# x of a chunk loaded in four groups of images, apart from one another, in place of two halves

## The chip, the cores and the metric

The kernel runs on one core of a Trainium2 chip. The metric is the device time of one execution in microseconds. SP is the engine that issues most transfers and computes nothing.

## The reference

```python
def reference(x, ...):                       # x: 32 images, 64 channels, 56 x 56, float32
    x = x + conv_ref(_ln_c(x), ...)          # layer norm over channels, sign, 3x3 conv with sign weights,
                                             # batch norm over images and places, clip to -1..1
    t = tokens of x                          # (32 images, 3136 places, 64 channels)
    t = t + ffn_ref(_ln_t(t), ...)           # 8 experts of three 64x64 layers, ReLU after the first two
    return t as x

def ffn_ref(x, ...):
    feat = jnp.mean(x, axis=0)               # mean over the 32 images, at each place
    w = softmax(feat @ Wr + br)              # one gate for each place and expert
    h = relu(bn(x @ W1[e] + b1[e])); h = relu(bn(h @ W2[e] + b2[e])); y = h @ Wo[e] + bo[e]
    return sum over e of y * w[e]
```

The gate of a place needs the mean over all images, so a chunk of places is worked on with all 32 images at once.

## The kernel before, in words

**First stage.** All images go through the first layer norm, the sign, the convolution and the statistics of its batch norm. The conv's result stays on the chip as `y`.

**Second stage.** 28 chunks (`chunk(k, s, first, left)` on each engine, from `body_of_chunks`). Chunk k holds rows k and 28 + k of all 32 images; the upper half of the rows is on partitions 0 to 63, the lower on 64 to 127, channels along the partitions. `s` is k % 2 and picks one of two buffers; `left` is the number of chunks that follow, 2 at most; `first` is true for k = 0. The images of a chunk are four groups (`g`) of 8. A chunk is 8 units (u), a unit is one half of the experts for one group, and a unit has six points, so a chunk has 48 positions. At fixed positions, given by the table `STEADY`, engines do steps for coming chunks: positions under 48 for chunk k + 2, from 48 on for chunk k + 1.

**The life of x.** SP loads x of chunk k + 2 into `xin[:, s]` while chunk k runs (`load_half`, L280; a half is two groups, and one call issues two transfers, one for each half of the partitions). The buffer holds chunk k's own values until GpSimd has used them, so each load waits for `x1g_done`, which `add_const` (L468: `o` = `xin` + the gates' constant) raises by one for each group. VectorE adds the conv's part into `xin` (`prep`, L1010) at positions 16, 21, 36 and 39 for groups 0 to 3; it waits for `x_loaded` at groups 0 and 2. TensorE centres x over channels (L634), ScalarE squares it into `spread`, TensorE sums (L642), ScalarE and VectorE make the inverse root `rs` (done at position 60, which is 12 of the next chunk).

**The other things that SP carries**, each with its wait: `spread_rs`, the row `rs` to memory (L293, two transfers) and back to all partitions (L297, four); `store(k, g)`, a group of the output (L314, two); `spread_gates`, the gates to memory and back (L304, L307). SP does them strictly in the order in which they are written.

**GpSimd** does `add_const` of groups 0 to 2, `add_upper(k - 1, 3)` (L474, L478: the sums into `o`), `add_const` of group 3 (which waits until `store(k - 1, 3)` has landed), `add_upper(k, 0)`, the two norm multiplications `xc` x `spread` (L446, which raise `u_done[0]` and `u_done[1]`), the feature (L455 to L460, the mean over images that the logits need), `add_upper(k, 1)` and `add_upper(k, 2)`.

**TensorE** runs, a unit, six steps of four concurrent 64x64 matmuls: layer 1 (L575), 2 (L599) and 3 (L614), each twice; at position 37 of a chunk the logits of the next one (L654), later its gates (L661, L675). **ScalarE** takes layer 1 out of PSUM (L801), **VectorE** layer 2 (L993). Once a chunk, near its start, ScalarE writes `gconst` (L846); its starts mark the chunks in the trace.

SP's order before:

```python
def chunk(k, s, first, left):
    if left > 1:
        sp.wait_ge(x1g_done, G * k + 2)
        load_half(k + 2, s, 0)
    if not first:
        store(k - 1, G - 1)
    if left:
        spread_rs(k + 1, 1 - s)
    if left > 1:
        sp.wait_ge(x1g_done, G * k + G)
        load_half(k + 2, s, 1)
    for g in range(G - 2):
        store(k, g)
```

Of the kernel before, what the change touches and what calls it, by code (L numbers as in the profile page):

```python
# [18 lines left out]
RP = H // 2  # L19
# [9 lines left out]
STEPS = 2  # L29
G = 4  # L30
BG = B // G
# [18 lines left out]
def metaformer_kernel(nc, x, cw, gamma, beta, Wr, br, W1, b1, g1, be1, m1, v1, W2, b2, g2, be2, m2, v2, Wo, bo, out):  # L50
    with ExitStack() as ctx:
        def sb(name, shape, dt, to=ctx):
            return to.enter_context(nc.sbuf_tensor(name, shape, dt))

        def sem(name):
            return ctx.enter_context(nc.semaphore(name))
# [40 lines left out]
        h = sb("h", [P, 2, 2, 2, NG], F32)  # L97
# [21 lines left out]
        xin = sb("xin", [P, 2, B, W], F32)  # L119
# [36 lines left out]
        d_bn = sem("d_bn")  # L156
        s_bn = sem("s_bn")

        x_loaded = [sem(f"x_loaded{p}") for p in range(STEPS)]
        t_done = sem("t_done")  # L160
        x1_done = sem("x1_done")
        centre_done = sem("centre_done")
# [13 lines left out]
        u_done = [sem(f"u_done{p}") for p in range(STEPS)]  # L176
# [13 lines left out]
        x1g_done = sem("x1g_done")  # L190
# [45 lines left out]
        def places_at(when, h):  # L236
            return [g for g in range(len(when)) if when[g] == h]
# [13 lines left out]
        with nc.Block() as block:  # L251
# [3 lines left out]
            def _(sp):  # L255
# [18 lines left out]
                for m in range(TWOS):  # L274
                    load_images(m)

                def load_half(q, s, p):
                    images = slice(2 * BG * p, 2 * BG * p + 2 * BG)
                    for h in range(2):
                        sp.dma_start(xin[64 * h:64 * h + 64, s, images], x[images, :, RP * h + q, :].rearrange("b c w -> c b w")).then_inc(x_loaded[p], 16)  # L280

                sp.wait_ge(a_stats, 1)
                for q in range(2):
                    for p in range(STEPS):
                        if q:
                            sp.wait_ge(x_loaded[p], 32)
                        load_half(q, q, p)

                def spread_rs(q, s):

                    sp.wait_ge(rs_done, q + 1)
                    for h in range(2):
                        sp.dma_start(rs_rows[s, h].rearrange("p i n -> (p i) n"), rs[h:h + 97:32, :]).then_inc(rs_kept, 16)  # L293
                    sp.wait_ge(rs_kept, 32 * q)
                    for p in range(STEPS):
                        for h in range(2):
                            sp.dma_start(spread[64 * h:64 * h + 64, p],  # L297
                                         rs_rows[s, h, p:p + 1].broadcast_to([C, 2, NG])).then_inc(rb_loaded[p], 16)

                def spread_gates(q, s):  # L300

                    sp.wait_ge(wT_done, q + 1)
                    for a in range(2):
                        sp.dma_start(gate_rows[s, :, a], wT[E * a:E * a + E, :]).then_inc(gates_kept, 16)  # L304
                    sp.wait_ge(gates_kept, 32 * q)
                    for hi in range(2):
                        sp.dma_start(wb[64 * hi:64 * hi + 64, s].rearrange("p n a w -> p (n a w)"),  # L307
                                     gate_rows[s, PAIRS * hi:PAIRS * hi + PAIRS].rearrange("(o n) a w -> o (n a w)", o=1).broadcast_to([C, NG])).then_inc(wb_loaded, 16)

                def store(k, g):  # L310
                    images = slice(BG * g, BG * g + BG)
                    sp.wait_ge(sum_done, G * k + g + 1)
                    for h in range(2):
                        sp.dma_start(out[images, :, RP * h + k, :].rearrange("b c w -> c b w"),  # L314
                                     o[64 * h:64 * h + 64, images]).then_inc(stored[g], 16)

                def chunk(k, s, first, left):
                    if left > 1:
                        sp.wait_ge(x1g_done, G * k + 2)
                        load_half(k + 2, s, 0)  # L320
                    if not first:
                        store(k - 1, G - 1)
                    if left:
                        spread_rs(k + 1, 1 - s)
                    if left > 1:
                        sp.wait_ge(x1g_done, G * k + G)
                        load_half(k + 2, s, 1)
                    for g in range(G - 2):
                        store(k, g)
                    if left:  # L330
                        spread_gates(k + 1, 1 - s)
                    store(k, G - 2)
                    if not left:
                        store(k, G - 1)
# [550 lines left out]
            def _(dve):  # L885
# [117 lines left out]
                def prep(at, q, s, h):  # L1003
                    Y, Z = L2_BANKS
                    for g in places_at(at.x1, h):
                        if g % 2 == 0:
                            dve.wait_ge(x_loaded[g // 2], 32 * q + 32)
                        dve.wait_ge(t_done, G * q + g + 1)
                        xg = xin[:, s, BG * g:BG * g + BG, :]
                        V.scalar_tensor_tensor(out=xg, in0=t[:, g].rearrange("p (b w) -> p b w", w=W), scalar=2.0, in1=xg,  # L1010
                                               op0=ALU.min, op1=ALU.add).then_inc(x1_done, 1)
# [94 lines left out]
```

## Time and profile before

| | us |
|---|---|
| median of 3 runs | 1347.0 (1344.51 to 1348.73) |
| the profiled execution | 1349.55 |
| its span | 1347.8 |
| TensorE matmul busy | 1287.7 (96%) |
| ScalarE busy | 881.1 (65%) |
| VectorE busy | 817.4 (61%) |
| GpSimd busy | 652.3 (48%) |
| mean granted TensorE clock | 0.989 |

The matmuls' ends are modelled and they overlap one another, so a busy TensorE is not one at its peak. The first stage ends, and the chunks begin, near 190 us. "Idle before" in a row is the engine's idle time just before the instructions of that row, and the name behind it is what ended it; "issue" stands where the profile shows nothing that it waited for.

### The profile page before, as it was taken

How to read it: one execution, taken by the hardware profiler on the slowest of the kernel's cores; microseconds unless marked ns; L12 is line 12 of the kernel's file. 1: busy time of each engine (PE TensorE's matmuls, PEld its weight loads, DVE VectorE, ACT ScalarE, POOL GpSimd, SP SyncE). 2: the span in 40 equal slices, each digit the busy share in tenths (PEclk: the TensorE clock that was granted, in tenths of full speed). 3: DMA queues.
4: the chain of work that ended last, by engine and by line, in shares of the span. 5: the costliest groups of instructions: out<-in, count | busy, mean ns of one | idle time of the engine just before them, and what ended most of it. 6: DMA issues, size and time to landing. Idle time of an engine off the chain costs nothing. (4 is left out here: it accounts for less than half of the span.)

```text
span 1347.8 us, 36336 instructions
## 1 busy us (share of the span) xinstructions
PE 1287.7 (96%) x14692; PEld 672.2 (50%) x14692; DVE 817.4 (61%) x1468; ACT 881.1 (65%) x1122; POOL 652.3 (48%) x580
## 2 busy tenths in 40 slices
PE   5999769999999999999999999999999999999997
PEld 3788525544445445444444544544445555534453
DVE  4444646666656566566665566665665656666654
ACT  5677656666666667666766666676666666666653
POOL 0142414554555544555644555445556455555453
PEclk9999979999999999999999999999999999999999
DMA  9897403343334442333442434423333334344221
GB/s 210 192 197 198 80 14 70 77 84 70 64 70 77 83 91 52 75 77 77 84 86 47 83 65 83 91 58 70 76 77 84 74 59 82 72 81 87 45 48 28
DMA packets 260976, 112.50 MB, mean 83 GB/s; under 512 B 241544, under 2 KB 245216, under 8 KB 260832
## 3 DMA queue, kind: packets, MB, share of 16 engines
q1 hardware_dynamic: 259568, 108.86, 39.5%
q0 software_dynamic: 1264, 1.61, 0.6%
q8 instruction: 104, 1.70, 0.6%
q14 instruction: 40, 0.33, 0.1%
HBM read 84.25 MB, written 26.17 MB: 82 GB/s over the span
## 5 line engine op out<-in xcount | busy, mean ns | idle before, releaser
L993 DVE SCALAR_TENSOR_TENSOR v<-ps,negb,wb 128x448 f32<-128x448 f32 x896 | 573.0, 678 | 413.2 <-PE ps L599 405.1
L801 ACT ACTIVATE h<-ps,bias 128x896 f32<-128x896 f32 x448 | 450.3, 1005 | 280.7 <-PE ps L575 278.0
L614 PE MATMUL ps<-v,wo 64*64 64x448 f32 x3584 | 472.7, 540 | 10.4 <-issue 9.7
L599 PE MATMUL ps<-h,w 64*64 64x448 f32 x3584 | 470.2, 540 | 4.2 <-issue 3.5
L575 PE MATMUL ps<-xc,w 64*64 64x448 f32 x3584 | 468.1, 540 | 6.4 <-issue 6.0
L474 POOL TENSOR_TENSOR sums<-sums 128x448 f32<-128x448 f32 x112 | 127.7, 1140 | 339.7 <-ACT sums L807 339.7
L599 PEld LDWEIGHTS ps<-h,w 64*64 64x64 f32 x3584 | 180.7, 133 | 178.9 <-issue 153.7
L614 PEld LDWEIGHTS ps<-v,wo 64*64 64x64 f32 x3584 | 173.7, 133 | 168.8 <-issue 148.1
L575 PEld LDWEIGHTS ps<-xc,w 64*64 64x64 f32 x3584 | 163.0, 132 | 183.9 <-issue 171.4
L468 POOL TENSOR_TENSOR o<-xin,gconst 128x448 f32<-128x448 f32 x112 | 125.1, 1137 | 206.4 <-DMA out<-o 95.0
L478 POOL TENSOR_TENSOR o<-o,sums 128x448 f32<-128x448 f32 x112 | 127.5, 1139 | 8.8
L446 POOL TENSOR_TENSOR xc<-xc,spread 128x896 f32<-128x896 f32 x54 | 113.3, 2112 | 20.0 <-DMA spread<-rs_rows 19.9
L536 PE MATMUL ps<-sgn,convw 64*64 64x392 bf16 x2304 | 116.8, 330 | 3.7 <-issue 3.7
L932 DVE BATCH_NORM_STATS2 stats<-y 128x6 f32<-128x392 f16 x128 | 66.2, 560 | 78.6 <-ACT y L768 78.5
L807 ACT ACTIVATE sums<-ps 128x896 f32<-128x896 f32 x112 | 101.4, 906 | 17.8 <-PE ps L614 17.8
L536 PEld LDWEIGHTS ps<-sgn,convw 64*64 64x64 bf16 x2304 | 91.0, 107 | 29.1 <-issue 8.9
L1010 DVE SCALAR_TENSOR_TENSOR xin<-t,xin 128x448 f32<-128x448 f32 x112 | 92.3, 825 | 1.6 <-ACT t L825 1.5
L825 ACT ACTIVATE t<-y,bn 128x448 f32<-128x448 f16 x112 | 83.5, 751 | 0.0
L768 ACT ACTIVATE y<-ps 128x784 f16<-128x784 f32 x64 | 52.8, 825 | 43.8 <-PE ps L536 43.8
L816 ACT ACTIVATE xc<-ps 128x896 f32<-128x896 f32 x54 | 49.6, 918 | 27.9 <-PE ps L634 27.9
L521 PE MATMUL ps<-xa,centre 64*64 64x392 f32 x512 | 63.2, 511 | 1.4 <-DMA xa<-in_x 1.3
L634 PE MATMUL ps<-xin,centre 64*64 64x448 f32 x432 | 59.0, 550 | 1.9 <-DVE xin L1010 1.1
(163 smaller groups left out, 626.5 us busy)
## 6 DMA issues: line engine op xcount, KB each, us to landing
xa<-in_x SPq DMA_DIRECT2D x128, 196.0 KB, 5.2
xin<-in_x SPq DMA_DIRECT2D x112, 224.0 KB, 5.0
out<-o SPq DMA_DIRECT2D x224, 112.0 KB, 2.5
spread<-rs_rows SPq DMA_DIRECT2D x108, 224.0 KB, 4.2
wb<-gate_rows SPq DMA_DIRECT2D x54, 112.0 KB, 2.8
rs_rows<-rs SPq DMA_DIRECT2D x54, 7.0 KB
gate_rows<-wT SPq DMA_DIRECT2D x54, 1.8 KB
rows<-in_L_ffn_g POOLq DMA_DIRECT2D x2, 256.0 KB, 5.2
```

Source lines behind the costliest of these rows:

```text
L446: nc.gpsimd.tensor_tensor(xc[:, s, p], xc[:, s, p], spread[:, p], ALU.mult).then_inc(u_done[p], 1)
L468: nc.gpsimd.tensor_tensor(o[:, images, :], xin[:, s, images, :], gconst[:, s:s + 1, :].broadcast_to([P, BG, W]), ALU.add).then_inc(x1g_don ...
L474: nc.gpsimd.tensor_tensor(sums[:, 0], sums[:, 0], sums[:, 1], ALU.add).then_inc(p_sum, 1)
L478: nc.gpsimd.tensor_tensor(og, og, sums[:, 0], ALU.add).then_inc(sum_done, 1)
L536: last = mm(ps[64 * high:64 * high + 64, CONV_BANKS[g % 2] + low, 0:NA], convw[rows_, tap, :], sgn[rows_, slot, top:top + KG, kx:kx + W], ...
L575: last = mm(ps[64 * two:64 * two + 64, L1_BANKS + ab, 0:NG], w1[half, P * q + C * two:P * q + C * two + C], xc[half, s, g // 2, ab ^ (g % ...
L599: last = mm(ps[64 * i:64 * i + 64, L2_BANKS[ab] + low, 0:NG], w2[rows_, Q + QUADS * i, :], h[rows_, u % 2, i, ab, :], start=True, stop=True)
L614: last = mm(ps[64 * par:64 * par + 64, ACC_BANKS + low, 0:NG], wo[rows_, 2 * Q + d, :], v[rows_, u % 2, par ^ (g % 2), d, :], start=(Q == ...
L801: A(h[:, u % 2, i], ps[:, L1_BANKS:L1_BANKS + 2, 0:NG], ACT.Relu, bias=bias[:, 0, q:q + 1]).then_inc(h_done[i], 1)
L807: A(sums[:], ps[:, ACC_BANKS:ACC_BANKS + 2, 0:NG], ACT.Copy).then_inc(sums_kept, 1)
L993: last = V.scalar_tensor_tensor(out=v[:, u % 2, ab, d, :].rearrange("p (b w) -> p b w", w=W), in0=ps[:, L2_BANKS[ab] + d, 0:NG].rearrange( ...
L1010: V.scalar_tensor_tensor(out=xg, in0=t[:, g].rearrange("p (b w) -> p b w", w=W), scalar=2.0, in1=xg, op0=ALU.min, op1=ALU.add).then_inc(x1 ...
```

## The change

x of a chunk is loaded by groups of 8 images (`load_group`, two transfers each) in place of halves of 16, each with a semaphore of its own. SP's order in a chunk is new: group 0 of chunk k + 2 as soon as `add_const(k, 0)` is through; the store of the last group of the chunk before; group 1; `spread_rs`; the store of group 0; group 2; group 3, which waits for `add_const(k, 3)` and also for the second norm multiplication of chunk k + 1 (`u_done[1]`, the last user of what `spread_rs` brings); the store of group 1; the rest as it was. VectorE's x1 step waits for each group's own load.

```diff
--- before.py
+++ after.py
@@ -156,7 +156,7 @@
         d_bn = sem("d_bn")
         s_bn = sem("s_bn")
 
-        x_loaded = [sem(f"x_loaded{p}") for p in range(STEPS)]
+        x_loaded = [sem(f"x_loaded{g}") for g in range(G)]
         t_done = sem("t_done")
         x1_done = sem("x1_done")
         centre_done = sem("centre_done")
@@ -274,17 +274,17 @@
                 for m in range(TWOS):
                     load_images(m)
 
-                def load_half(q, s, p):
-                    images = slice(2 * BG * p, 2 * BG * p + 2 * BG)
+                def load_group(q, s, g):
+                    images = slice(BG * g, BG * g + BG)
                     for h in range(2):
-                        sp.dma_start(xin[64 * h:64 * h + 64, s, images], x[images, :, RP * h + q, :].rearrange("b c w -> c b w")).then_inc(x_loaded[p], 16)
+                        sp.dma_start(xin[64 * h:64 * h + 64, s, images], x[images, :, RP * h + q, :].rearrange("b c w -> c b w")).then_inc(x_loaded[g], 16)
 
                 sp.wait_ge(a_stats, 1)
                 for q in range(2):
-                    for p in range(STEPS):
+                    for g in range(G):
                         if q:
-                            sp.wait_ge(x_loaded[p], 32)
-                        load_half(q, q, p)
+                            sp.wait_ge(x_loaded[g], 32)
+                        load_group(q, q, g)
 
                 def spread_rs(q, s):
 
@@ -315,18 +315,25 @@
                                      o[64 * h:64 * h + 64, images]).then_inc(stored[g], 16)
 
                 def chunk(k, s, first, left):
+
+                    if left > 1:
+                        sp.wait_ge(x1g_done, G * k + 1)
+                        load_group(k + 2, s, 0)
+                    if not first:
+                        store(k - 1, G - 1)
                     if left > 1:
                         sp.wait_ge(x1g_done, G * k + 2)
-                        load_half(k + 2, s, 0)
-                    if not first:
-                        store(k - 1, G - 1)
+                        load_group(k + 2, s, 1)
                     if left:
                         spread_rs(k + 1, 1 - s)
+                    store(k, 0)
                     if left > 1:
+                        sp.wait_ge(x1g_done, G * k + 3)
+                        load_group(k + 2, s, 2)
                         sp.wait_ge(x1g_done, G * k + G)
-                        load_half(k + 2, s, 1)
-                    for g in range(G - 2):
-                        store(k, g)
+                        sp.wait_ge(u_done[1], k + 3)
+                        load_group(k + 2, s, 3)
+                    store(k, 1)
                     if left:
                         spread_gates(k + 1, 1 - s)
                     store(k, G - 2)
@@ -1003,8 +1010,7 @@
                 def prep(at, q, s, h):
                     Y, Z = L2_BANKS
                     for g in places_at(at.x1, h):
-                        if g % 2 == 0:
-                            dve.wait_ge(x_loaded[g // 2], 32 * q + 32)
+                        dve.wait_ge(x_loaded[g], 32 * q + 32)
                         dve.wait_ge(t_done, G * q + g + 1)
                         xg = xin[:, s, BG * g:BG * g + BG, :]
                         V.scalar_tensor_tensor(out=xg, in0=t[:, g].rearrange("p (b w) -> p b w", w=W), scalar=2.0, in1=xg,
```

On SP, one chunk with two or more chunks after it stood so before. `xin` is the load of x, `out` a store of one group, `rs_rows` and `spread` the inverse root to memory and back, `gate_rows` and `wb` the gates:

```order
L280 DMA xin<-in_x 64x16x56 x2
L314 DMA out<-o 64x8x56 x2
L293 DMA rs_rows<-rs 4x448 x2
L297 DMA spread<-rs_rows 64x896 x4
L280 DMA xin<-in_x 64x16x56 x2
L314 DMA out<-o 64x8x56 x4
L304 DMA gate_rows<-wT 8x56 x2
L307 DMA wb<-gate_rows 64x448 x2
L314 DMA out<-o 64x8x56 x2
```

The same chunk on SP in the changed kernel:

```order
L280 DMA xin<-in_x 64x8x56 x2
L314 DMA out<-o 64x8x56 x2
L280 DMA xin<-in_x 64x8x56 x2
L293 DMA rs_rows<-rs 4x448 x2
L297 DMA spread<-rs_rows 64x896 x4
L314 DMA out<-o 64x8x56 x2
L280 DMA xin<-in_x 64x8x56 x4
L314 DMA out<-o 64x8x56 x2
L304 DMA gate_rows<-wT 8x56 x2
L307 DMA wb<-gate_rows 64x448 x2
L314 DMA out<-o 64x8x56 x2
```

Group 1 has moved behind the first store, and groups 2 and 3 behind the store that follows the spread; the row of four `xin` is both of them, with a wait between.

## Rows read from the trace of the kernel before

**Rows 1.** The page, busy time of each engine.

```profile
PE 1287.7 (96%) x14692; PEld 672.2 (50%) x14692; DVE 817.4 (61%) x1468; ACT 881.1 (65%) x1122; POOL 652.3 (48%) x580
```

**Rows 2.** The page, a DMA queue: packets, MB, share of 16 engines.

```profile
q8 instruction: 104, 1.70, 0.6%
```

**Rows 3.** Groups by line: busy us, mean ns, idle before and its releasers.

```profile
L614 PE MATMUL ps<-v,wo 64*64 64x448 f32 x3584 | 472.7, 540 | 10.4 <-issue 9.7 <-ACT sums L807 0.5
L599 PE MATMUL ps<-h,w 64*64 64x448 f32 x3584 | 470.2, 540 | 4.2 <-issue 3.5 <-ACT vareps L829 0.4
L575 PE MATMUL ps<-xc,w 64*64 64x448 f32 x3584 | 468.1, 540 | 6.4 <-issue 6.0
```

**Rows 4.** Line L846: duration ns min/median/max, first and last start us.

```profile
L846 ACT ACTIVATE gconst<-ps x28: 206/208/211, 192.3 to 1300.4; 128x56 f32<-128x56 f32 x28
```

**Rows 5.** Timeline of ScalarE, three chunks' starts: start us, us, instruction.

```profile
317.85 0.21 ACT L846 ACTIVATE gconst<-ps 128x56 f32<-128x56 f32 x1
...
357.10 0.21 ACT L846 ACTIVATE gconst<-ps 128x56 f32<-128x56 f32 x1
...
400.43 0.21 ACT L846 ACTIVATE gconst<-ps 128x56 f32<-128x56 f32 x1
```

**Rows 6.** Timeline of TensorE at 382 us, in brackets the idle before.

```profile
381.87 0.98 PE L614 MATMUL ps<-v,wo 64*64 64x448 f32 x8 [1.96 <-issue]
```

**Rows 7.** Windows: us, busy (count) of PE, PEld, DVE, ACT, POOL, clock, DMA share, GB/s.

```profile
322.00:323.00 1.00, 1.00 (x16) 0.36 (x12) 0.89 (x2) 0.49 (x2) 0.00 (x0) 1.00 0.96 200
...
378.00:379.00 1.00, 1.00 (x19) 0.54 (x16) 0.99 (x2) 0.00 (x0) 1.00 (x2) 1.00 1.35 188
...
380.00:381.00 1.00, 0.00 (x0) 0.00 (x0) 1.00 (x2) 0.88 (x2) 0.87 (x2) 1.00 0.10 13
...
383.00:384.00 1.00, 1.00 (x12) 0.60 (x8) 0.00 (x0) 0.83 (x1) 0.92 (x2) 0.50 0.00 0
```

**Rows 8.** Timeline of SP in the chunk that starts at 317.85.

```profile
320.40 1.73 SPq L280 DMA_DIRECT2D xin<-in_x  x2
326.80 1.30 SPq L314 DMA_DIRECT2D out<-o  x2
329.45 1.10 SPq L293 DMA_DIRECT2D rs_rows<-rs  x2
331.71 2.48 SPq L297 DMA_DIRECT2D spread<-rs_rows  x4
334.24 1.34 SPq L280 DMA_DIRECT2D xin<-in_x  x2
335.87 13.16 SPq L314 DMA_DIRECT2D out<-o  x4
```

**Rows 9.** Line L280 (issue ns, first and last, landing); the page's stores, us to landing.

```profile
L280 SPq DMA_DIRECT2D xin<-in_x x112: 595/672/1423, 136.9 to 1238.4; - x112
...
DMA to landing us min/median/max: 3.5/5.0/6.5
...
out<-o SPq DMA_DIRECT2D x224, 112.0 KB, 2.5
```

**Rows 10.** Timeline of VectorE, the same chunk: groups 1, 2 and 3 of x.

```profile
335.14 1.18 DVE L1010 SCALAR_TENSOR_TENSOR xin<-t,xin 128x448 f32<-128x448 f32 x1
...
347.17 1.03 DVE L1010 SCALAR_TENSOR_TENSOR xin<-t,xin 128x448 f32<-128x448 f32 x1
...
350.83 0.61 DVE L1010 SCALAR_TENSOR_TENSOR xin<-t,xin 128x448 f32<-128x448 f32 x1
```

**Rows 11.** Timeline of GpSimd, the same chunk: sum of group 0, norms, end of the feature.

```profile
334.70 1.14 POOL L478 TENSOR_TENSOR o<-o,sums 128x448 f32<-128x448 f32 x1
336.43 4.29 POOL L446 TENSOR_TENSOR xc<-xc,spread 128x896 f32<-128x896 f32 x2 [0.59 <-DMA spread<-rs_rows]
...
344.98 0.42 POOL L460 TENSOR_TENSOR feat<-feat 128x112 f32<-128x112 f32 x1
```

**Rows 12.** Timeline of TensorE, the same chunk: the logits.

```profile
347.98 0.27 PE L654 MATMUL ps<-wr,feat 64*56 64x8 f32 x5
```

More of the change, by code:

```diff
@@ L318, in chunk @@
                     if left > 1:
-                        sp.wait_ge(x1g_done, G * k + 2)
-                        load_half(k + 2, s, 0)
+                        sp.wait_ge(x1g_done, G * k + 1)
+                        load_group(k + 2, s, 0)
                     if not first:
                         store(k - 1, G - 1)
+                    if left > 1:
+                        sp.wait_ge(x1g_done, G * k + 2)
+                        load_group(k + 2, s, 1)
                     if left:
                         spread_rs(k + 1, 1 - s)
+                    store(k, 0)
                     if left > 1:
+                        sp.wait_ge(x1g_done, G * k + 3)
+                        load_group(k + 2, s, 2)
                         sp.wait_ge(x1g_done, G * k + G)
-                        load_half(k + 2, s, 1)
-                    for g in range(G - 2):
-                        store(k, g)
+                        sp.wait_ge(u_done[1], k + 3)
+                        load_group(k + 2, s, 3)
+                    store(k, 1)
                     if left:
```

## The prediction

> **What bounds the kernel now.** I read the page first: the TensorE is busy for 96% of the span [rows 1], so whatever the change does to the transfers counts only if it moves the TensorE. The part on queues comes next: beside SP's queue there is one, q8, that carries 104 packets of instructions, 1.70 MB, some 16 KB each [rows 2]. The TensorE has by far the longest program, 14692 matmuls and as many weight loads [rows 1], and 29384 instructions in at most 104 blocks are over 280 a block, so most of these blocks must be its code (an inference: the profile does not say whose they are). The grouping by line then shows the three layers' matmuls idle 21 times for 19.2 us in all (9.7 + 3.5 + 6.0) behind "issue", which is no wait that the profile knows [rows 3]. Of semaphore waits these groups have next to none.
>
> The chunk's length says how much is lost. The row of gconst (one a chunk) starts at 192.3 the first and at 1300.4 the last time of 28 [rows 4]: 1108.1 / 27 = 41.04 us a chunk. A clean chunk takes 357.10 - 317.85 = 39.25 us, the next one 400.43 - 357.10 = 43.33 [rows 5]. The same work is done in both. So the 27 intervals lose about 27 x (41.04 - 39.25) = 48 us (the first and the last differ a little in what they hold; I take it as a bound).
>
> Where does the long one lose it? Its TensorE stands for 1.96 us before 381.87, released by "issue" [rows 6]. In the slices before, the DMA engines are at 1.35 of their mean share in 378 to 379; while the TensorE stands, in 380 to 381, they are at 0.10. Two microseconds later the granted clock is 0.50, that is 1.2 GHz in place of 2.4, for some 3 us [rows 7]. I read this so: a block of code was queued behind a long burst of transfers, came late, the TensorE ran dry, and once it was followed by a lower clock. The burst is what SP issues in one go. Of the clean chunk: rs_rows at 329.45, four spread transfers from 331.71, the second half of x from 334.24, the store of group 0 from 335.87 [rows 8]. A store transfer is 112 KB [rows 9]; a spread one (64 partitions of 896 floats) and one of a half of x (64 of 16 images of 56 floats) are 224 KB. That is 4 x 224 + 2 x 224 + 2 x 112 = 1568 KB. The first half of x, alone at 320.40, is moved at a share of 0.96 in 322 to 323 [rows 7, 8], and the chunk loses nothing by it.
>
> **The change part by part, all in the clean chunk's times.**
>
> *More issues.* Eight x transfers of 112 KB a chunk for four of 224 KB, same bytes and same 224-byte pieces. One issue takes 672 ns at the median [rows 9]; a store of 112 KB takes the same, 1.30 us for two [rows 8]. So SP spends 4 x 0.67 = 2.7 us a chunk more. It lies in SP's waits: nothing is lost but what is queued behind, below. The x of the first two chunks is loaded from 136.9 on [rows 9], during the first stage, 55 us before the first gconst at 192.3 [rows 4]: nothing.
>
> *Group 1 goes behind the store of group 3 of the chunk before.* The store is issued from 326.80 to 328.10; group 1 then from 328.10 to 329.44, 8 us later than now. VectorE takes it at 335.14 [rows 10]. What a 112 KB load needs from issue to landing is not in the trace: 2.5 us is the store's of that size, 5.0 the load's of twice that [rows 9]. I take 3.5, between, since an HBM read of half the bytes should lie nearer the store; the second transfer, issued at 328.77, lands by 332.3, with 331.3 and 333.8 as ends. Even the late end leaves 1.3 us. Cost nothing, covered by that slack. VectorE's two more waits a chunk (groups 1 and 3) are met before they are reached.
>
> *rs_rows has group 1 ahead of it.* SP is free again at 329.44 and rs is ready at 329.45, so the issue itself is not moved. But rs_rows, and through its landing the four spreads, now have 224 KB in front. In 322 to 323 a load of x moves 200 GB/s [rows 7], at which 224 KB (0.229 MB) are 1.15 us: 0 to 1.2 us, I take 1. The norm multiplications on GpSimd start at 336.43, at the release of the spread [rows 11], and the feature sum ends at 344.98 + 0.42 = 345.40. TensorE's logits, which want it, run at 347.98 [rows 12]. Slack 2.6 us: 1 us is hidden. Against it, the spread no longer shares the engines with the second half of x. Net on the path: nothing.
>
> *Groups 2 and 3.* Store 0 is issued from 335.87 (it can go no earlier: its sum ends at 334.70 + 1.14 [rows 11]), then group 2 from 337.2 to 338.5; the norms end at 336.43 + 4.29 = 340.72 and let out group 3, issued until 342.1. With 5.0 us to landing as the worst, group 2 is there by 343.0 and group 3 by 346.4; they are taken at 347.17 and 350.83 [rows 10]. Slack 4 us each. Behind group 3 SP holds the store of group 1, whose sum GpSimd makes only after the feature, so after 345.40: nothing.
>
> *The burst.* This is the term that counts. After the spread come 224 KB of store and 224 KB of group 2, issued at the rate of 0.67 us per 112 KB, and group 3 only after 340.7. So the 1568 KB become 896 KB, then 448 KB that trickle, then 224 KB apart, and the stretch with the engines over-full ends with the spread, about 2 to 3 us earlier. A block wanted in that tail is no longer late; one wanted during the spread is as late as now. I take half of the visible idle of the matmuls: 0.5 x 19.2 = 9.6 us. The ends: nothing below (all of the lateness could come from the spread), and 48 us of loss above, of which the tail of the burst can hardly hold more than half, 24.
>
> Here two rules of the skill speak against the term. The Trainium skill, Runtime: NRT & Kernel Launch, Instruction fetch mechanics, has the sequencer fetch 16 KiB blocks of 256 instructions through a queue of its own, "mostly hidden". The size agrees with q8's packets [rows 2]; "hidden" does not agree with the 1.96 us gap, if that gap is a fetch. The Trainium skill, DMA: Bandwidth & Descriptors, Queues, rings and completion order, says that each engine takes turns between queue rows packet by packet; by it a backlog in SP's row would hold the code up by a packet or so, and this term would be 0. Rows 6 and 7 speak for more; no row shows the fetch itself.
>
> *Tail.* From chunk 26 on no x is loaded, and the code is the old one in order: nothing.
>
> **Sum.** The profiled execution took 1349.55 us (span 1347.8), 2.55 above the median of the runs, 1347.0. 1349.55 - 9.6 = 1339.95; against the median, 1347.0 - 9.6 = 1337.4. I say 1337. A measurement of this kernel can tell 0.3%, 4 us, from nothing.
>
> **The rivals.**
>
> *The burst is not what makes the code late, or the spread alone is.* For it: the clean chunk has the same burst and no gap, and the skill's rule of turns. Against it: the gap stands right behind the 1.35 slices. Time: 1347, within 4 us. Chance 0.25.
>
> *The tail is worth more than I take.* If every gap goes, the hidden part of each and the lower clock with it: 1347 - 24 = 1323. This is the low part of the forecast's own case, as likely as a fifth of it.
>
> *Group 1 comes too late (slower).* Place: VectorE at L1010, position 21 of 48 in the chunk, between two v products that TensorE's third layer waits for. Behind it VectorE has nothing else to do and the TensorE drains within a step. It decides once group 1 lands after 335.14, that is 6.4 us after its second issue, or when the store of group 3 is itself held up by 3 us. Price: each microsecond beyond, in 26 chunks; at half a microsecond 13 us, 1360. For it: 8 us of lead are given away, and read and store share the engines. Against it: the longest of all 112 landings of the doubled size is 6.5 us [rows 9]. Chance 0.08.
>
> *More and denser issues hold up the code in a new place (slower).* Store 3, group 1 and rs_rows are now issued without a break from 326.8 to 330.6, and a block wanted there may be late where it wasn't. Price: one gap of half a microsecond in every second chunk, 13 x 0.5 = 6.5 us, with the gain of the tail lost: 1353. For it: the total issue time grows by 2.7 us a chunk. Against it: the DMA engines are mostly idle in that stretch. Chance 0.09.
>
> **How the numbers follow.** The forecast's case has 0.58, "no effect" 0.25, the two slower ones 0.17 together. Where the gain happens it is 5 to 25 us, so 1322 to 1342; the range goes on to the whole of "no effect", 1351, and a microsecond into the second slower rival: 1322 to 1352. What lies outside is a gain over 25 us (0.05) and group 1 late (0.08), with part of the other. Faster by over 0.3%: 0.58; within: 0.25; slower: 0.17.
>
> **What would show it.** Right: the period of gconst falls from 41.04 towards 40.7; the idle of the three matmul groups behind "issue" falls from 19.2 to about 10; slices after the spread show a share below 1.1; no idle of VectorE behind the DMA of x; norms start no later than 1 us after now. Wrong: the same 19 us of idle at other places (second or fourth case); a row of VectorE's L1016 (the x1 step's new line) waiting for the DMA of x (third case); GpSimd's norms over 2.6 us later, with the TensorE idle at the logits.

## The result and the profile after

| | before | changed |
|---|---|---|
| median of 6 runs | 1345.76 us | 1333.27 us |
| lowest to highest | 1342.81 to 1348.73 | 1330.46 to 1336.47 |
| profiled execution, its span | 1349.55, 1347.8 | 1334.76, 1332.6 |

The ratio is 0.9906, with a 95% interval of 0.9887 to 0.9924: 12.5 us less, where 9.6 were forecast. The runs of before are measured anew beside the changed kernel, so their median differs a little from the 1347.0 of the table above.

The page of the changed kernel: busy time of each engine, and the queue of instructions.

```profile
PE 1281.6 (96%) x14692; PEld 661.5 (50%) x14692; DVE 819.3 (61%) x1468; ACT 881.1 (66%) x1122; POOL 652.5 (49%) x580
...
q8 instruction: 104, 1.70, 0.5%
```

The count of matmuls is the same. The span fell by 15.2 us, and the TensorE's busy time by 6.1 of them (1287.7 in [rows 1]), so its idle time fell by 9.1, from 60.1 to 51.0. Of these 15.2 us some 2 are scatter: the profiled execution of before was 3.8 us above its median, the changed one 1.5.

The three layers' matmuls, grouped by line (busy us, mean ns of one, idle us before them and its releaser):

```profile
L621 PE MATMUL ps<-v,wo 64*64 64x448 f32 x3584 | 469.7, 540 | 4.7 <-issue 3.9
L606 PE MATMUL ps<-h,w 64*64 64x448 f32 x3584 | 466.5, 539 | 3.1 <-issue 2.4
L582 PE MATMUL ps<-xc,w 64*64 64x448 f32 x3584 | 463.3, 540 | 5.1 <-issue 4.6
```

Against [rows 3] the idle time behind "issue" is 10.9 us in place of 19.2. The line of gconst, its first and last start, and three chunks' starts in ScalarE's timeline:

```profile
L853 ACT ACTIVATE gconst<-ps x28: 205/208/211, 192.1 to 1285.2; 128x56 f32<-128x56 f32 x28
```

```profile
316.23 0.21 ACT L853 ACTIVATE gconst<-ps 128x56 f32<-128x56 f32 x1
...
355.47 0.21 ACT L853 ACTIVATE gconst<-ps 128x56 f32<-128x56 f32 x1
...
395.18 0.21 ACT L853 ACTIVATE gconst<-ps 128x56 f32<-128x56 f32 x1
```

(1285.2 - 192.1) / 27 = 40.49 us a chunk, where it was 41.04 [rows 4]. The clean chunk is as before, 39.24 us; the one behind it, 43.33 before [rows 5], takes 39.71. By the bound that the prediction uses, 27 x (40.49 - 39.24) = 34 us of loss are left of 48.

SP's timeline in the chunk that starts at 316.23 (start us, us, instruction):

```profile
317.67 1.31 SPq L280 DMA_DIRECT2D xin<-in_x  x2
325.18 1.30 SPq L314 DMA_DIRECT2D out<-o  x2
326.52 1.34 SPq L280 DMA_DIRECT2D xin<-in_x  x2
327.91 1.12 SPq L293 DMA_DIRECT2D rs_rows<-rs  x2
330.25 2.60 SPq L297 DMA_DIRECT2D spread<-rs_rows  x4
334.24 1.34 SPq L314 DMA_DIRECT2D out<-o  x2
335.62 4.72 SPq L280 DMA_DIRECT2D xin<-in_x  x4
```

Behind the four transfers of the spread, issued until 332.85, SP is still until 334.24; then it issues six transfers of 112 KB over 6.1 us, where before two of 224 and two of 112 KB came at once [rows 8]. The windows over the same phase of the next chunk, the one that lost 4 us before (columns as in [rows 7]):

```profile
373.40:374.40 1.00, 1.00 (x16) 0.40 (x12) 1.00 (x2) 1.00 (x2) 0.51 (x2) 1.00 0.96 233
374.40:375.40 1.00, 1.00 (x16) 0.43 (x12) 0.73 (x2) 0.40 (x2) 1.00 (x1) 1.00 0.62 119
375.40:376.40 1.00, 1.00 (x16) 0.33 (x8) 0.31 (x1) 0.95 (x1) 1.00 (x2) 1.00 0.76 153
376.40:377.40 1.00, 1.00 (x17) 0.56 (x16) 0.96 (x2) 0.00 (x0) 1.00 (x1) 1.00 0.78 145
```

The last slice is the one that stood at 1.35 before [rows 7]; it is at 0.78. The TensorE's 1.96 us of idle [rows 6] and the stretch at a clock of 0.50 behind it are gone from this chunk.

### The profile page after: what moved, and what is told of

Read it like the earlier page. It is cut to its first block and busy times, and to the rows that moved or that the text cites. A ratio compares the mean times of both kernels' runs of the same rounds, so it can differ in the third digit from the quotient of the medians.

```text
span 1332.6 us, 36530 instructions
## 1 busy us (share of the span) xinstructions
PE 1281.6 (96%) x14692; PEld 661.5 (50%) x14692; DVE 819.3 (61%) x1468; ACT 881.1 (66%) x1122; POOL 652.5 (49%) x580
## 5 line engine op out<-in xcount | busy, mean ns | idle before, releaser
L582 PE MATMUL ps<-xc,w 64*64 64x448 f32 x3584 | 463.3, 540 | 5.1 <-issue 4.6
L543 PEld LDWEIGHTS ps<-sgn,convw 64*64 64x64 bf16 x2304 | 82.9, 107 | 37.1 <-issue 8.8
L1016 DVE SCALAR_TENSOR_TENSOR xin<-t,xin 128x448 f32<-128x448 f32 x112 | 95.0, 848 | 1.6 <-ACT t L832 1.5
L462 POOL TENSOR_TENSOR feat<-xc 128x896 f32<-128x896 f32 x27 | 56.6, 2097 | 3.6
```

Of the source, the lines that this page charges most:

```text
L543: last = mm(ps[64 * high:64 * high + 64, CONV_BANKS[g % 2] + low, 0:NA], convw[rows_, tap, :], sgn[rows_, slot, top:top + KG, kx:kx + W], ...
L582: last = mm(ps[64 * two:64 * two + 64, L1_BANKS + ab, 0:NG], w1[half, P * q + C * two:P * q + C * two + C], xc[half, s, g // 2, ab ^ (g % ...
```

## The experiments

Two theories were open. **Late code:** blocks of the TensorE's instructions come late behind a burst of transfers, so the places of the gaps follow the TensorE's count of instructions, and what helps is a thinner burst. **Something else:** the smaller transfers by themselves, the place of group 1, or the spread alone. Each run is compared with runs of the kernel before on the same chip, whose medians lay between 1344.7 and 1349.0 us.

### Size without place, place without size

The first kernel takes the changed one's four groups and puts them where the halves stood.

```diff
 if left > 1:
-    sp.wait_ge(x1g_done, G * k + 1)
+    sp.wait_ge(x1g_done, G * k + 2)
     load_group(k + 2, s, 0)
+    load_group(k + 2, s, 1)
 if not first:
     store(k - 1, G - 1)
-if left > 1:
-    sp.wait_ge(x1g_done, G * k + 2)
-    load_group(k + 2, s, 1)
 if left:
     spread_rs(k + 1, 1 - s)
+if left > 1:
+    sp.wait_ge(x1g_done, G * k + G)
+    load_group(k + 2, s, 2)
+    load_group(k + 2, s, 3)
 store(k, 0)
-if left > 1:
-    sp.wait_ge(x1g_done, G * k + 3)
-    load_group(k + 2, s, 2)
-    sp.wait_ge(x1g_done, G * k + G)
-    sp.wait_ge(u_done[1], k + 3)
-    load_group(k + 2, s, 3)
 store(k, 1)
```

> Four groups, each with its semaphore, but issued where the halves were: groups 0 and 1 together at the chunk's start, groups 2 and 3 together right behind the spread, then the store of group 0. Size changed, place not. Theory A (a long burst of transfers behind the spread makes TensorE's blocks of code late): the burst has the same bytes and is only stretched by 1.3 us of issue, so the time is within 0.3% of the kernel before, 1342 to 1350, and the idle of the three layers' matmuls behind issue stays near 19 us. Rival B (smaller transfers are what helps, wherever they stand): as fast as the changed kernel, 1333, idle near 11 us.

Measured: 1346.89 us, ratio 0.9988 [0.9974, 1.0003]. The matmuls idle 8.6 + 4.2 + 6.8 = 19.6 us behind "issue", as before. The size of the transfers alone gives nothing that these runs can measure.

The second leaves the kernel before its halves and moves the second one behind the norms.

```diff
     spread_rs(k + 1, 1 - s)
+store(k, 0)
 if left > 1:
     sp.wait_ge(x1g_done, G * k + G)
+    sp.wait_ge(u_done[1], k + 3)
     load_half(k + 2, s, 1)
-for g in range(G - 2):
-    store(k, g)
+store(k, 1)
```

> The kernel before with one edit: the second half of x goes out behind the store of group 0 and after the second norm multiplication (u_done[1]); still two halves, the first half where it was. Place changed, size not. Theory A: all or more of the gain, 1329 to 1336, since no load of x lies in the burst of the spread; the 448 KB then make a burst of 2.2 us by themselves, which has cost nothing at the chunk's start. Rival B (size is what helps): 1342 to 1350. The second half lands some 5 us after 24 us in the chunk, group 2 is taken at 29.3: no wait of VectorE.

Measured: 1341.22 us, ratio 0.9957 [0.9942, 0.9971], outside what was expected; the idle behind "issue" is 17.0 us. The old gaps are mostly gone, and new ones stand elsewhere. The TensorE's timeline of this kernel, in the chunk that starts at 475.74:

```profile
505.18 0.59 PE L600 MATMUL ps<-h,w 64*64 64x448 f32 x2 [1.22 <-issue]
```

Its windows in front of that gap:

```profile
501.00:502.00 1.00, 1.00 (x17) 0.70 (x12) 0.86 (x2) 0.62 (x2) 0.98 (x1) 1.00 1.27 232
...
504.00:505.00 1.00, 0.00 (x0) 0.00 (x0) 0.00 (x0) 1.00 (x2) 0.92 (x2) 1.00 0.00 0
```

and what SP issued for it:

```profile
498.60 1.34 SPq L280 DMA_DIRECT2D xin<-in_x  x2
```

So 448 KB of x issued in 1.34 us, with the DMA engines at a share of 0.01 or less in the three slices before 500, already make a slice of 1.27, with a late block behind it. A burst need not be the long one behind the spread.

### The changed kernel's own steps, one at a time

Without the wait for the norms ahead of group 3:

```diff
     sp.wait_ge(x1g_done, G * k + G)
-    sp.wait_ge(u_done[1], k + 3)
     load_group(k + 2, s, 3)
```

> The changed kernel without the wait of group 3 for the norm multiplication: group 3 goes straight behind group 2. Theory A: groups 2 and 3 still stand behind the store of group 0 and are issued at 0.67 us per 112 KB from 19.4 us in the chunk on, when the spread is nearly landed; a little of the gain is lost, 1334 to 1340. If the wait is what matters most, the time goes back to 1343 or more; if it matters nothing, 1333 within 2 us.

Measured: 1338.47 us, 0.9938 [0.9921, 0.9956]. Its interval just touches the changed kernel's. By the two ratios the wait is worth some 4 us, and this is no more than likely.

With store 0 behind the first norm, and groups 2 and 3 together behind the second:

```diff
+if left:
+    sp.wait_ge(u_done[0], k + 3)
 store(k, 0)
 if left > 1:
-    sp.wait_ge(x1g_done, G * k + 3)
-    load_group(k + 2, s, 2)
     sp.wait_ge(x1g_done, G * k + G)
     sp.wait_ge(u_done[1], k + 3)
+    load_group(k + 2, s, 2)
     load_group(k + 2, s, 3)
```

> The changed kernel with the stretch behind the spread emptied further: the store of group 0 waits for the first norm multiplication, group 2 as well as group 3 for the second. Theory A (a long burst makes code blocks late): nothing but the spread is in the engines from 14 to 20.6 us in the chunk, so the gaps at 19 to 22 us shrink, 1326 to 1332; but groups 2 and 3 are then one burst of 448 KB at 23 to 27 us, and in the kernel with the second half behind the norms (1341) such a burst made new gaps at 28 to 29 us. If that weighs more, 1334 to 1340. If the store and group 2 do nothing, the time of the changed kernel, about 1335 beside a before of 1348.

Measured: 1333.13 us, 0.99 [0.9884, 0.9917], the same as the changed kernel; none of the further gain that the late-code theory allowed (1326 to 1332) came. SP's timeline of this kernel:

```profile
497.57 2.66 SPq L280 DMA_DIRECT2D xin<-in_x  x4
```

These are the same 448 KB behind the norms as in the kernel with the half moved, but as four issues over 2.66 us, not two over 1.34; that one took 1341.2 us. The pair differs in the first half and in store 0 too, so it only suggests that the rate of issue is what counts here, and that size and place work together.

With group 1 right behind group 0, ahead of the store of group 3:

```diff
     load_group(k + 2, s, 0)
-if not first:
-    store(k - 1, G - 1)
-if left > 1:
     sp.wait_ge(x1g_done, G * k + 2)
     load_group(k + 2, s, 1)
+if not first:
+    store(k - 1, G - 1)
```

> The changed kernel with group 1 back where the first half was, straight behind group 0 and ahead of the store of group 3; the rest as changed. Theory A: the gain comes from what stands behind the spread, so this part of the change is worth nothing: 1333 within 3 us, ratio 0.989 to 0.993. If group 1 in front of rs_rows costs something, it is a little faster; if the loads' being apart everywhere is what counts, it loses 3 us or more.

Measured: 1335.96 us, 0.9925 [0.991, 0.994]: not to be told from the changed kernel. The place of group 1 is worth nothing that these runs can measure.

### Does the gap follow the program or the transfers?

The kernel before, with 128 more instructions on the TensorE ahead of the chunks (about half a block, as the traces show below):

```diff
+for _ in range(128):
+    pe.sem_inc(shift, 1)
 pe.wait_ge(a_stats, TWOS + 1)
```

> The kernel before with 128 further instructions on TensorE (an increment of a semaphore that nobody reads) ahead of the batch norm's statistics, where TensorE waits anyway. Nothing else is touched. If the gaps are blocks of TensorE's own code that come late, their places follow TensorE's instruction count: a chunk has about 900 of its instructions, three and a half blocks of 256, so 128 more swap the chunks. In the kernel before chunks 2, 4 and 6 are long (41.4, 43.3, 42.1 us) and chunks 3, 5 and 7 short (39.2, 40.1, 40.3); here 3, 5 and 7 are the long ones, with idle of 1 us or more behind issue at 24 to 25 us in the chunk, and 4 and 6 are near 39.5. If the gaps come from data, from another engine or from one phase of the transfers against each other, the same chunks stay long. The total within 0.5% of the kernel before in either case.

Measured: 1365.55 us, 1.0122 [1.0099, 1.0145]. The time missed the expectation (within 0.5% of the kernel before), since the increments themselves took time: the first gconst comes at 206.4, 14 us later than before. The chunks' starts in its ScalarE timeline:

```profile
332.23 0.21 ACT L849 ACTIVATE gconst<-ps 128x56 f32<-128x56 f32 x1
...
373.70 0.21 ACT L849 ACTIVATE gconst<-ps 128x56 f32<-128x56 f32 x1
...
413.22 0.21 ACT L849 ACTIVATE gconst<-ps 128x56 f32<-128x56 f32 x1
...
455.89 0.20 ACT L849 ACTIVATE gconst<-ps 128x56 f32<-128x56 f32 x1
```

Before, the chunk behind the three starts of [rows 5] ended here:

```profile
440.47 0.21 ACT L846 ACTIVATE gconst<-ps 128x56 f32<-128x56 f32 x1
```

The first of these intervals, 39.25 us before [rows 5], is now 41.47, and the second, 43.33 before, is 39.52; the third, 440.47 - 400.43 = 40.04 before, is 42.67, with this row 25 us into it:

```profile
438.51 0.59 PE L602 MATMUL ps<-h,w 64*64 64x448 f32 x2 [1.70 <-issue]
```

|---|---|---|---|---|
| before, the gap of [rows 6] | 379.91 to 381.87 | 379.14 | 380.38 | 1.49 |
| changed | 1022.51 to 1023.97 | 1021.49 | 1022.67 | 1.30 |
| half moved | 503.96 to 505.18 | 502.50 | 503.91 | 1.27 |
| 128 instructions more | 436.81 to 438.51 | 435.69 | 437.12 | 1.39 |

From 205 to 1280 us the kernel before has 16 idle stretches of the TensorE of over 0.3 us, 16.9 us in all. Each ends 1.25 to 1.72 us after a q8 packet has landed. Count the TensorE's instructions from zero (weight loads, matmuls, semaphore instructions and the rest, by their starts): the matmul behind each of the 16 gaps stands at a multiple of 256, plus 13. From one gap to the next the count of q8 packets grows by one for every 256 instructions. The 11 gaps of the changed kernel in the same stretch stand at the same remainder. So do 20 of the 21 of the kernel with 128 more from 220 us on, with the 128 counted, and the last is one off. So in the chunks q8 carries the TensorE's code, a block is 256 instructions, and these gaps are waits for the next block. The 14 us by which the chunks began later do not explain that.

Why some blocks are late and others not can be read too. Over the chunks of the kernel before, a block lands 1.6 us ahead of its first instruction at the median and 1.2 at the least. For 57 of 94 blocks it is less than 1.8 us, as at the gaps: most blocks arrive with nothing to spare. Compare the 92 blocks of the two kernels from 210 us on, one by one. Sixteen were fetched 19 to 24.5 us into a chunk in the kernel before, in or just behind the burst:

| | those 16, before | the same, changed | the other 76, before | the same, changed |
|---|---|---|---|---|
| mean DMA share in the 2 us ahead of the packet | 1.14 | 0.76 | 0.29 | 0.30 |
| packet starts, us after the block before began to run | 9.74 | 9.07 | 8.50 | 8.50 |
| the packet's own length, us | 1.25 | 1.09 | 1.13 | 1.10 |
| us saved from block to block, in all | | 11.5 | | 3.2 |

The change lets these 16 blocks land some 0.8 us earlier in their turn, and through them it wins most of its time: 11.5 of 14.7 us.

### What the transfers cost, and what the code costs

The kernel before, without the second half of x from chunk 2 on. VectorE waits in its place for GpSimd's use of the old values (this part is not shown), so groups 2 and 3 are computed from old x:

```diff
-if left > 1:
-    sp.wait_ge(x1g_done, G * k + G)
-    load_half(k + 2, s, 1)
...
```

> The kernel before without the transfers of the second half of x for chunks 2 on (VectorE takes what stands in the buffer, after the same use of it by GpSimd as before): groups 2 and 3 of these chunks are computed from old values. It prices all that the second half costs by being moved at all. Theory A: no load behind the spread and none after the norms: 1326 to 1333, at least as fast as the changed kernel. If it stays at 1343 or more, the second half is not what delays the code, and the gain of the change has another source.

Measured: 1335.31 us, 0.9918 [0.9901, 0.9934]. Leaving the second half out gives no more than the change does. So the change wins back what these transfers cost, as far as these runs can tell.

The changed kernel with the second pair of spread transfers behind the landing of the first:

```diff
 for p in range(STEPS):
+    if p:
+        sp.wait_ge(rb_loaded[0], 32 * q)
     for h in range(2):
```

> The changed kernel with the spread itself in two parts: the two transfers of the second half of the spread are issued only when those of the first have landed, some 2 us later than now. Theory A: the burst that is left, 896 KB in one go, becomes two of 448 KB, so the gaps at 19 to 22 us shrink, 1325 to 1332. Price: the second norm starts up to 1.5 us later and the feature ends at 28.5 to 29 us in the chunk, before the logits at 30. If that slack is not enough, TensorE waits at the logits and the time is 1336 or more. If bursts are not the cause: as the changed kernel or slower.

Measured: 1337.64 us, 0.9934 [0.992, 0.9948]: 4 us more than the changed kernel, with intervals that just overlap, and the branch of the expectation in which the slack is not enough. The idle behind "issue" fell to 3.0 + 1.4 + 3.9 = 8.3 us. The second norm and with it the feature now come late, and the TensorE waits at the logits, a wait that the changed kernel does not have. From this kernel's list of waits (us in total, times, longest):

```profile
PE ps L663 <- POOL feat L469: 1.8, 4, 1.0
```

The slack of 2.6 us at the logits [rows 11, 12] was spent there. These 1.8 us do not account for the whole loss; the rest stays open, the more so as this profile is of the fastest of the kernel's six runs (1334.4).

The changed kernel without the spread at all (the norm multiplies by what the buffer holds, and GpSimd waits for rs only):

```diff
-for p in range(STEPS):
-    for h in range(2):
-        sp.dma_start(spread[...], rs_rows[...]).then_inc(rb_loaded[p], 16)
...
-pool.wait_ge(rb_loaded[p], 32 * q)
+pool.wait_ge(rs_kept, 32 * q)
```

> The changed kernel without the spread's four transfers (896 KB a chunk): the norm multiplies by what stands in the buffer, so the FFN's input is not normalized. It prices the burst that the change leaves. Theory A: with 896 KB gone the gaps at 19 to 22 us in the chunk vanish: 1312 to 1326. If the time stays within 3 us of the changed kernel's, the gaps that are left do not come from the spread.

Measured: 1321.36 us, 0.9825 [0.9803, 0.9848]. The idle behind "issue" is 1.6 + 0.8 + 3.8 = 6.2 us. The spread's transfers are thus worth 12 us of what is left.

Now from the other side, the code: ahead of its matmuls the TensorE marks the steps of the layers (of layer 3 every other one) with an increment (l1_free, l2_free, l3_free; 40 a chunk, 1120 in all) that no engine waits for. The changed kernel without them:

```diff
-pe.sem_inc(l1_free, 1)
...
-pe.sem_inc(l2_free, 1)
...
-pe.sem_inc(l3_free, 1)
```

> The changed kernel without three semaphore increments of TensorE that nobody waits for (l1_free, l2_free, l3_free; 40 a chunk of about 900 instructions), no other edit. If gaps are code blocks that come late, 4% fewer instructions mean 4% fewer blocks and the next block is wanted some 0.5 us later: fewer and shorter gaps, 1326 to 1332 beside a before of 1346 to 1348. If TensorE's code is not the matter, 1333 within 2 us; an increment costs TensorE nothing that shows between matmuls. It could also be slower, if the increments keep a wait from being held at the weight load.

Measured: 1300.1 us, 0.9664 [0.9644, 0.9684], far better than expected, and better than both kernels. The same groups of its page:

```profile
L618 PE MATMUL ps<-v,wo 64*64 64x448 f32 x3584 | 433.9, 539 | 1.1 <-DVE v L997 0.7
L581 PE MATMUL ps<-xc,w 64*64 64x448 f32 x3584 | 432.7, 540 | 2.2 <-ACT h L805 2.1
L604 PE MATMUL ps<-h,w 64*64 64x448 f32 x3584 | 429.7, 537 | 0.3 <-ACT vareps L833 0.3
```

and its line of gconst:

```profile
L850 ACT ACTIVATE gconst<-ps x28: 205/206/212, 192.1 to 1253.6; 128x56 f32<-128x56 f32 x28
```

"issue" no longer releases any of the three groups. A chunk takes (1253.6 - 192.1) / 27 = 39.31 us, so nearly every one is a clean one. A clean chunk of the changed kernel, with the increments in it, takes 39.24 too: what they cost is not their own time.

The edit does more than take out 1120 instructions. In the trace a mark is a semaphore instruction of its own that also holds one or two of the waits ahead of its matmuls. Without the marks these waits must stand elsewhere: 1155 weight loads hold a wait, where 35 did, and other semaphore instructions hold the rest, so the TensorE's instructions fall by 400 only (31272 to 30872). From the first gconst to the last, the blocks of code and the TensorE's pauses at them are these:

| | before | changed | changed, no marks | before, no marks |
|---|---|---|---|---|
| packet starts, us after the block before began to run, median | 8.5 | 8.6 | 3.3 | 3.6 |
| block landed ahead of its first instruction, us, median (shortest) | 1.6 (1.2) | 1.6 (1.2) | 7.2 (3.7) | 6.6 (4.0) |
| longest pause from one matmul's start to the next, within 4 instructions of a block's first, us, summed over the blocks | 46.0 | 34.9 | 12.7 | 12.8 |

Without the marks the code is fetched about 5 us earlier, and no block is late. The last column is the last kernel of this section.

The changed kernel ran once more beside these:

> The changed kernel as it is, beside the two others on the same chip: ratio 0.989 to 0.993 to the kernel before.

Measured: 1333.79 us, 0.9914 [0.9893, 0.9935], with 4.8 + 2.8 + 5.5 = 13.1 us of idle behind "issue". The same kernel showed 10.9 in its first profile: such sums vary by some 2 us from one execution to the next.

Last, the kernel before without the same three increments:

> The kernel before (halves, the burst behind the spread) without the three semaphore increments of TensorE that nobody waits for. The changed kernel without them took 1300 and nearly all its chunks 39.2 us, with no idle behind issue left. Theory A: all that the change gives goes through late code, so with the lateness gone the old order is as fast: 1298 to 1303, ratio 0.965 to 0.969. If the order of the loads has another worth: 1306 or more. If the long burst still makes code late even so: between, with idle behind issue at 20 to 25 us in the chunk.

Measured: 1300.19 us, 0.9627 [0.9606, 0.9649]. Its windows right behind the spread, in the chunk that starts at 313.98:

```profile
334.00:335.00 1.00, 1.00 (x16) 0.35 (x12) 0.47 (x1) 0.78 (x1) 0.42 (x1) 1.00 1.32 197
335.00:336.00 1.00, 1.00 (x16) 0.55 (x16) 0.81 (x2) 0.00 (x0) 0.92 (x1) 1.00 1.28 182
```

The burst stands as it did in [rows 7], and the time is the same as with the four groups, 1300.2 against 1300.1. (The two ran on different chips, where the kernel before took 1349.0 and 1344.7; by the ratios the old order is even ahead by 0.4%, with intervals that just overlap.) Once the code is no longer late, the change is worth nothing; its 12.5 us were won by way of late code.

## Why the prediction was right, step by step

**The bound.** Right. Blocks of the TensorE's code that come late cost this kernel about the 48 us that the prediction bounded: without the marks it is 1349.0 - 1300.2 = 48.8 us faster. That most blocks are the TensorE's was an inference, and it holds: every gap of over 0.3 us from 205 us to the last chunk stands at the start of a block of 256, just behind a packet of q8. Its working does not hold. It divides all matmuls and weight loads by all packets, over 280 a block, but a block is 256. The first stage runs in a loop: only 6 of the 104 packets come before the first gconst at 192.3, for 6161 of the TensorE's instructions.

**The burst.** Right in mechanism, too small by a quarter: 9.6 us forecast, 12.5 measured. The mis-sized factor is the basis, not the half: the visible idle fell by 8.3 us (19.2 to 10.9; by the second profile of the changed kernel 6.1), near the half, but a late block costs more than the idle that it shows. In the chunk of [rows 6] 1.96 us of idle went with 4.08 us of length: the starts of two matmuls are 2.50 us apart there, and 3.41 us at a clock of 0.50 follow, which cost half of that, 1.7 us. Such a stretch is the exception: from 200 us to the last gconst it is the only one of the kernel before, and the changed kernel has none. Most of the rest is pauses that the modelled ends of the matmuls cover, so that they count as busy. The pauses at the blocks' first instructions fell by 11.1 us (46.0 to 34.9), where the idle of the three groups fell by 8.3. Over the kernel 9.1 us of the fall were idle and 6.1 busy; with the marks gone, another 9.2 and 24.4 (busy 1281.6 to 1257.2, span 1332.6 to 1299.0, by the pages), and the pauses at the blocks fell by another 22.2. That the half of 19.2 came near the measured gain is in part luck: of the 33 us by which the pauses at the blocks could fall (46.0 to 12.8), the change won a third.

**Where in the burst.** The forecast gave the second half of x a share and the spread another. The kernel without the second half (1335.3) and the one without the spread (1321.4) give these shares their sizes: all of 12.5 us, and 12 us more, which the change does not touch. The slices after the spread fell below 1.1 in 23 of the first 25 chunks, as said; in the other two, two slices each are above. The two kernels that changed only the size or only the place show that the term needed both: 1346.9, 1341.2, and 1333.3 together.

**More issues, and group 1 behind the store.** Nothing that can be measured, as said. The landing of 112 KB, taken as 3.5 us between 2.5 and 5.0, is a measured 2.8 (line L280 of the changed kernel; on [rows 9] it was 5.0 for twice the size):

```profile
DMA to landing us min/median/max: 2.6/2.8/4.6
```

VectorE took group 1 at 333.51 with no idle before it, 5.7 us after its last issue ended:

```profile
333.51 1.18 DVE L1016 SCALAR_TENSOR_TENSOR xin<-t,xin 128x448 f32<-128x448 f32 x1
```

No wait of VectorE for x is in the list of waits. The rival with group 1 too late (0.08) falls by this and by the run with group 1 early.

**rs_rows behind group 1.** The norms were put at 1 us later, and came no later. GpSimd's timeline:

```profile
334.85 4.14 POOL L453 TENSOR_TENSOR xc<-xc,spread 128x896 f32<-128x896 f32 x2 [0.64 <-DMA spread<-rs_rows]
...
343.25 0.42 POOL L467 TENSOR_TENSOR feat<-feat 128x112 f32<-128x112 f32 x1
```

The norms start 18.62 us into the chunk (334.85 - 316.23), where it was 18.58 (336.43 - 317.85, [rows 5, 11]). The error cost nothing, as the slack would have covered it.

**Denser issues in a new place.** This rival (0.09) falls for the changed kernel, whose idle fell in all three groups. Its mechanism is real all the same: in the kernel with the half moved, new gaps appeared where there had been none.

## What to carry to other kernels

Idle time behind "issue" on the engine with the longest program, at places that no wait explains, is code that comes late: look in the trace for a packet of the instruction queue that lands a microsecond or two ahead of the end of each gap, look for a burst of transfers ahead of it, and test with some idle instructions in front, which move the gaps. Spread such a burst out by issuing smaller transfers behind waits that space them, but only within the slack of what they feed. Before that, drop semaphore increments between the matmuls that nobody waits for, and see where their waits go; here that was worth 49 us where pacing the transfers was worth 12.5, and it made the pacing worthless.

## What the runs showed that was not expected

- 128 semaphore increments in a row on the TensorE start 0.15 us apart, from 155.29 to 174.92, and put the chunks off by 14 us (first gconst at 206.4 in place of 192.3). In that kernel's list of waits they stand as one:

```profile
PE ps L560 <- issue: 18.4, 1, 18.4
```

- The 40 increments a chunk that nobody waits for, with the waits that they hold, cost 33 us of the changed kernel's 1333 and 49 of the kernel before's, and nothing in a clean chunk.
- 448 KB issued in 1.34 us, with the DMA engines at rest before, were enough for a late block: 1.22 us of idle that ended some 5 us after the issue did.
- Half of what late code costs or more stands in the profile as busy time of the TensorE: with the marks gone its busy time fell by 24.4 us of 33.6, at the same count of matmuls and nearly the same mean duration (537 to 540 ns).
- In the kernels with the marks a block of the TensorE's code lands 1.6 us ahead of its first instruction at the median, so a delay of under a microsecond already stops the engine.
